# Graph layer on one core: VectorE's first gate of a node block moved up, one eviction per turned tile pair, and the first edge group started among the counting tiles

## What is computed

```python
h = relu(layernorm(x))                                  # every node
w = relu(edge_feat @ W_fc1) @ W_fc2                     # every edge, 224 weights
xs, xv = (h_s @ W_nl0)[dst], (h_v @ W_nl1)[dst]         # gathered node rows
tp = products of w, xs, xv and the edge's direction     # 96 scalars, 128 vectors
agg = segment_sum(tp, src) / 32                         # messages added per node
out_s = agg_s @ W_out_s + h_s @ W_skip0
out_v = agg_v @ W_out_v + h_v @ W_skip1
out = x + concat(silu(out_s[:, :64]), sigmoid(out_s[:, 64:96]) * out_v)
```

## Time and profile before

| | us |
|---|---|
| median of 3 runs | 1428.96 (1420.41 to 1432.81) |
| the profiled execution | 1418.56 |
| its span | 1416.7 |
| counting tiles, about | 0 to 195 |
| edge groups, about | 195 to 660 |
| start of the node stage, about | 660 to 700 |
| node rounds, about | 700 to 1408 |

### The profile page before, as it was taken

The page is one execution under the profiler, slowest core; times in us unless marked ns, Lnnn a source line. Parts: engine busy times, 40 slices in busy tenths (PEclk is TensorE's granted clock), DMA queues, the critical chain, the costliest instruction groups (busy, mean ns, idle before and its releaser), DMA issues.

```text
span 1416.7 us, 33669 instructions
## 1 busy us (share of the span) xinstructions
PE 1222.7 (86%) x8853; PEld 1006.4 (71%) x8853; DVE 1115.9 (79%) x4156; ACT 1028.6 (73%) x2594; POOL 854.8 (60%) x1077
## 2 busy tenths in 40 slices
PE   4999979988888888895798898899898999888896
PEld 2555547777777777785677787777787888777786
DVE  7999998777777767778287887788888888787875
ACT  2777766777667767774477786678788888777785
POOL 5555477666667666640675665576666666665661
PEclk9999989999999999998699999999999999999999
DMA  5000013333333333331487787788888888787873
GB/s 197 1 0 0 0 38 92 96 92 87 91 94 96 95 83 90 96 89 48 99 250 226 227 235 218 200 242 243 234 244 238 251 241 250 214 230 222 235 206 103
DMA packets 90933, 212.41 MB, mean 150 GB/s; under 512 B 15031, under 2 KB 56282, under 8 KB 90879
## 3 DMA queue, kind: packets, MB, share of 16 engines
q1 hardware_dynamic: 62462, 155.23, 34.0%
q0 software_dynamic: 28416, 56.56, 18.5%
HBM read 127.73 MB, written 84.00 MB: 149 GB/s over the span
## 4 chain that ended last, share of the span: by engine, by line
PE 42%; ACT 17%; issue 12%; DVE 9%; another core or an unknown queue 5%; ACTq 1%; DVEq 0%; POOL 0%; DMA 0%; POOLq 0%
PE bank L1387 9%; ACT nn L1177 8%; PE bank L1379 7%; PE bank L1401 6%; PE bank L1307 4%; PE bank L1336 3%; PE bank L1391 2%; PE bank L1324 2%; PE bank L1320 2%; DVE n_stat L855 2%; PE bank L1322 2%; ACT tpt L1136 2%; PE bank L1291 2%; PE bank L1292 1%
## 5 line engine op out<-in xcount | busy, mean ns | idle before, releaser
L574 POOL DMA_INDIRECT mg<-messages,slot_m x392 | 456.6, 1165 | 281.5 <-ACT slot_m L1199 115.4
L1177 ACT ACTIVATE nn<-xb,n_bias,n_rstd 128x160 f32<-128x160 f32 x686 | 340.5, 651 | 10.9 <-DVE n_bias L656 10.7
L1387 PE MATMUL bank<-wsk_a,nt_a 128*128 128x160 f32 x1568 | 300.1, 315 | 9.9 <-DVE ob L946 7.5
L946 DVE SCALAR_TENSOR_TENSOR ob<-sg,bank 128x128 f32<-128x128 f32 x588 | 132.4, 279 | 154.3 <-ACT ob L1193 150.6
L502 POOL DMA_INDIRECT xg<-x,dst_g x200 | 208.4, 1042 | 61.8 <-issue 56.7
L1387 PEld LDWEIGHTS bank<-wsk_a,nt_a 128*128 128x128 f32 x1568 | 233.5, 197 | 14.9 <-issue 12.7
L1379 PE MATMUL bank<-ident,nn 128*128 128x128 f32 x784 | 149.4, 314 | 78.8 <-ACT nn L1177 55.7
L1379 PEld LDWEIGHTS bank<-ident,nn 128*128 128x128 f32 x784 | 110.8, 210 | 134.7 <-issue 76.3
L855 DVE BATCH_NORM_STATS2 n_stat<-xb 128x6 f32<-128x160 f32 x784 | 200.8, 309 | 1.4 <-DMA xb<-x 1.4
L1401 PE MATMUL bank<-mg,hot 64*128 64x192 f32 x1568 | 186.3, 355 | 8.9 <-issue 4.5
L1184 ACT ACTIVATE nt_a<-bank 128x512 f32<-128x512 f32 x196 | 117.1, 598 | 84.3 <-PE bank L1380 77.8
(11 more groups left out here) (179 smaller groups left out, 2633.8 us busy)
## 6 DMA issues: line engine op xcount, KB each, us to landing
xb<-x SPq DMA_DIRECT2D x97, 640.0 KB
out_dram<-ob SPq DMA_DIRECT2D x97, 640.0 KB
messages<-msg SPq DMA_DIRECT2D x50, 390.6 KB
mg<-messages,slot_m POOLq DMA_INDIRECT x392
ef<-edge_feat_t SPq DMA_DIRECT2D x50, 125.0 KB
xg<-x,dst_g POOLq DMA_INDIRECT x200
xb<-x SPq DMA_DIRECT2D x1, 420.0 KB
out_dram<-ob SPq DMA_DIRECT2D x1, 420.0 KB
```

The costliest lines, as they stand in the source:

```text
L574: pool.indirect_dma_start(mg[:, m, k, :], None, messages[:, :], bass.IndirectOffsetOnAxis(ap=slot_m[:, m, k:k + 1], axis=0)).then_inc(n.g[ ...
L946: last = dve.scalar_tensor_tensor(out=o[:, :, S + V * j:S + V * j + V], in0=sg[:, h, :, :], scalar=1.0, in1=z[:, :, part], op0=ALU.add, op ...
L1177: last = act.activation(nn[:, u % 2, h, :, g % 4], xb[:, u, g, :], ACT.Relu, bias=n_bias[:, u // U, c:c + 1], scale=n_rstd[:, u // U, c:c ...
L1387: pe.matmul(z[:, t, 0:F], nt_a[:, h, t * P:(t + 1) * P], wsk_a[:], start=(t % 2 == 0), stop=False, skip_group_check=True)
```

## The change

It has five parts.

- **VectorE, node stage.** In `round_n` the call `gate(i, u, 0)` moves from behind the statistics (and, in root rounds, behind the whole root chain) to the place between the one-hots and the statistics.
- **ScalarE, both stages.** The turned rows get one PSUM range of five 128-column slots and one SBUF tile, so one copy of 640 columns (`nt`) replaces 512 plus 128, and one of 625 (`ht`) replaces 500 plus 125.
- **First edge group.** Its turn, hidden layer, weights and row products move into the last 20 counting tiles, in PSUM bank 3, which is free there. ScalarE's three evictions go with them.
- **GpSimd.** The four gathers of edge group 2 are issued among the first 20 counting tiles, not after the last.
- **VectorE, edge stage.** `table()` moves from round 0 to round 3.

```diff
@@ node stage, VectorE
+                        if every:
+                            places(i)
                         if extract:
                             seed(j, w)
+                        gate(i, u, 0)
+                        if extract:
                             if measure:
                                 stats_n(s, v, 0, 1)
                             root_a(j, w, 0)
...
-                        if every:
-                            places(i)
-                        gate(i, u, 0)
                         if extract:
                             shift_n(j, w)
@@ node stage, ScalarE
-                        act.activation(nt_a[:, h, :], q_t[h], ACT.Relu)
-                        act.activation(nt_z[:, h, :], q_tz[h], ACT.Relu).then_inc(n.ht, 1)
+                        act.activation(nt[:, h, :], q_t[h], ACT.Relu).then_inc(n.ht, 1)
@@ edge stage, ScalarE
-                        act.activation(ht[:, c, :], p_t, ACT.Copy)
-                        act.activation(hz[:, c, :], p_tz, ACT.Copy).then_inc(e_ht, 1)
+                        act.activation(ht[:, c, :, :], p_t, ACT.Copy).then_inc(e_ht, 1)
@@ edge stage, VectorE
-                    if isinstance(q, int) and q == 0:
+                    if isinstance(q, int) and q == 3:
                         table()
@@ counting tiles, GpSimd
+                        if isinstance(t, int) and t < BR:
+                            gathers(2, 2, [k // BATCH])
...
-                gathers(2, 2)
@@ counting tiles, ScalarE
+                    if isinstance(t, int) and t == NT - BR:
+                        act.wait_ge(e_t, 1)
+                        act.activation(ht[:, 0, :, :], f_t, ACT.Copy).then_inc(e_ht, 1)
+                    if isinstance(t, int) and t == NT - BR + 8:
+                        act.wait_ge(e_h1, 1)
+                        act.activation(hid[:], f_h, ACT.Relu).then_inc(e_hid, 1)
+                    if isinstance(t, int) and t == NT - 3:
+                        act.wait_ge(e_w, 1)
+                        act.activation(w_sb[:, 0, :, :], f_w, ACT.Copy).then_inc(e_wsb, 1)
@@ counting tiles, PE
+                    if isinstance(t, int) and t == NT - BR:
+                        turn_first()
+                    if isinstance(t, int) and t == NT - BR + 12:
+                        hidden_first()
                 edge_tiles(pe, tile_b)
                 for t in range(NT - BLOCK, NT):
                     table(t, t % BR, t // BR)
+                    if t == NT - 8:
+                        weights_first()
+                rows_first()
                 pe.wait_ge(b_free, 3)
```

More of the change, by code:

```diff
@@ L199, in gnn_layer @@
         hot = sb("hot", [P, 2, BPM, P])
-        nt_a = sb("nt_a", [P, 2, 4 * P])
-        nt_z = sb("nt_z", [P, 2, P])
+        nt = sb("nt", [P, 2, 5 * P])
         sg = sb("sg", [P, 2, 4, V])
@@ L496, in _, with gathers @@
                                    pattern=[[1, ET]], channel_multiplier=-1).then_inc(s_const, 1)
[L497 removed]
+                def gathers(q, b, tiles=range(GE)):
                     wait(pool, e_norm, q - D + 1)
@@ L500, in gathers @@
                     pool.sem_inc(s_held, 1)
-                    for t in range(GE):
+                    for t in tiles:
                         pool.indirect_dma_start(xg[:, b, t, :], None, x[:, :],
@@ L781, in products @@
                 def products(p, c):
+                    first = isinstance(p, int) and p == 0
+                    rows = f_x if first else p_x
+                    row_s, row_v = rows[:, :, 0:S], rows[:, :, S:F].rearrange("p t (i k) -> p t i k", i=3)
                     w = w_sb[:, c, :, :]
@@ L1129, in round_e @@
                     c = b % 2
+                    first = isinstance(q, int) and q == 0
                     def take(t):
@@ L1163, in round_e @@
                     take(3)
-                    if within(q):
+                    if within(q) and not first:
                         act.wait_ge(e_w, q + 1)
@@ L1257, in table, with turn_first, hidden_first, weights_first @@
                               skip_group_check=True).then_inc(b_tab, 1)
+                idt = ident[0:ET, 0:ET]
+                def turn_first():
+                    pe.wait_ge(e_norm, 1)
+                    for t in range(GE):
+                        pe.transpose(f_t[:, t, :], hn[:, 0, 0:P, t], idt)
+                    pe.transpose(f_t[:, GE, :], hn[:, 0, P:F, :], idt).then_inc(e_t, 1)
+                def hidden_first():
+                    pe.wait_ge(s_w, 16 * len(weight_loads))
+                    pe.wait_ge(e_f[0], 16)
+                    pe.wait_ge(e_ht, 1)
+                    pe.matmul(f_h, wfc1[:], ef[:, 0, :], start=True, stop=True).then_inc(e_h1, 1)
+                def weights_first():
+                    pe.wait_ge(e_hid, 1)
+                    for t in (0, 2, 1, 3):
+                        part = slice(EF * (t // 2), EF * (t // 2) + EF)
+                        last = pe.matmul(f_w[:, t, :], hid[part, t % 2 * ET:(t % 2 + 1) * ET], wfc2[part, :],
+                                         start=True, stop=True)
+                    last.then_inc(e_w, 1)
+                def rows_first():
+                    pe.wait_ge(e_wsb, 1)
+                    rows(f_x, 0).then_inc(e_xs, 1)
+                def rows(to, c):
+                    for t in range(GE):
+                        pe.matmul(to[:, t, 0:P], ht[:, c, t, :], wnl_a[:],
+                                  start=(t % 2 == 0), stop=True, skip_group_check=True)
+                        if t % 2 == 1:
+                            j = t // 2
+                            last = pe.matmul(to[:, 2 * j:2 * j + 2, P:F], ht[:, c, GE, :],
+                                             wnl_z[:, 2 * V * j:2 * V * j + 2 * V],
+                                             start=False, stop=True, skip_group_check=True)
+                    return last
                 count(0, tri_before, 0).then_inc(b_pre, 1)
@@ L1328, in weights @@
                     def weights(tiles):
-                        if not within(q):
+                        if not within(q) or first:
                             return
@@ L1356, in round_e @@
                     turn(0, p + 1, 1 - c)
-                    if within(q):
+                    if within(q) and not first:
                         wait(pe, e_px, q)
-                        for t in range(GE):
-                            pe.matmul(p_x[:, t, 0:P], ht[:, c, t * ET:(t + 1) * ET], wnl_a[:],
-                                      start=(t % 2 == 0), stop=True, skip_group_check=True)
-                            if t % 2 == 1:
-                                j = t // 2
-                                last = pe.matmul(p_x[:, 2 * j:2 * j + 2, P:F], hz[:, c, :],
-                                                 wnl_z[:, 2 * V * j:2 * V * j + 2 * V],
-                                                 start=False, stop=True, skip_group_check=True)
-                        last.then_inc(e_xs, 1)
+                        rows(p_x, c).then_inc(e_xs, 1)
                 groups(pe, round_e)
```

43 lines of the change are left out of this document (20 added, 23 removed).

## The result

The change made the kernel slower: 1473.01 us (1467.57 to 1477.99, 4 runs) against 1428.36 (1420.41 to 1432.81, 4 runs), a ratio of 1.032 with a 95% interval of 1.026 to 1.038. The profiled execution took 1477.99 us with a span of 1476.2, 59.5 us more than the span before.

A forecast was written before the change was run, and what follows sets the result against it. No engine is full, so waits decide, mostly in the node stage. Terms -7.5 - 24 - 4.9 - 3 - 2 = -41.4 us from 1418.56 give 1377.2; with half the median's 10.4 us offset kept, 1382 us, range 1366 to 1415.

The forecast's parts named there:

- The pauses: Node stage: ScalarE's idle times of 3.0 to 4.2 us behind long gate waits lose three quarters of 32 us, -24 us.
- The pauses stay: Rival: the gate waits go, but ScalarE's pauses come from something else and remain; 1411 us, chance 0.28.
- VectorE becomes late: Rival: in root rounds the waiting gate delays shift and `nn`, and such waits bring more pauses; 1466 us, chance 0.05.
- The gate waits: Node stage: PE's 19 waits of `skip` for VectorE's gate, 6.9 us, go with their hand-overs, -7.5 us.
- The merged eviction: Node stage: one ScalarE eviction for two saves 0.05 us on the loop in each of 98 rounds, -4.9 us.
- Edge groups and seam: Edge groups: merged eviction, -3 us; seam between counting tiles and edge groups: `products` of group 0 near 203 us, -2 us.

The follow-up runs named there:

- held gathers: Kernel before, with GpSimd's gathers of block j also waiting for VectorE's one-hots of block j-2: 1313.9 us, ratio 1.000, on a chip without pauses.
- the gate alone: Kernel before with only the gate's move: 1304.36 us (ratio 0.993) on a chip without pauses, 1475.31 us (1.026) on one with pauses.
- all but the gate: Changed kernel with the gate's move undone: 1310.25 us (ratio 0.998) on a chip without pauses, 1462.92 us (1.014) on one with pauses.

## Why the prediction was wrong

**The pauses: the step that failed.** I read them as set off by PE's long wait for the gate, because each stood behind such a wait, and took three quarters of 32 us as a gain. The waits went, and the pauses went from 6 to 17. With the disturbed and the undisturbed chips side by side the term can be sized, from first to last slot row. Undisturbed, this is 645.9 us for the change and 663.8 for the kernel before with held gathers, which is as fast as the kernel before:

```profile
L1201 ACT ACTIVATE slot_m<-slots_i x98: 189/206/228, 612.2 to 1276.0; 128x4 int32 x80, 128x4 int32<-128x4 int32 x18
```

So the pauses cost the change 762.9 - 645.9 = 117.0 us, and the kernel before 708.8 - 663.8 = 45.0. The term is +72 instead of -24. On a chip with pauses, but without gathers, the change takes 1336.8 - 681.4 = 655.4; the 9.5 us over 645.9 lie at the start of the node stage, where the stop behind the first 16 gathers is. If the kernel before loses as much there, 35.5 us are left for its rounds, where I had 32: the size before was about right, its cause was not.

The rows of before could have told me. A pause stood behind each of six gate waits of 0.45 to 0.95 us (three of them stand under another releaser, though `skip` starts 0.15 us behind the gate's end), but others of 0.48 and 0.51 had none of 3 us or more. The `skip` at 860.04 has one behind it, the one at 1154.32 has not:

```profile
860.04 0.78 PE L1387 MATMUL bank<-wsk_a,nt_a 128*128 128x160 f32 x4 [0.45 <-DVE ob L946]
...
1154.32 0.78 PE L1387 MATMUL bank<-wsk_a,nt_a 128*128 128x160 f32 x4 [0.51 <-DVE ob L946]
```

And the earlier trace rows have 30.5 us of idle time of `ht` under "remote" in the edge groups, where there is no gate. Only one core runs, and on the chip without pauses the changed kernel has no such row. The long gate wait and the pause were two things in one place, behind a root round. That the root chain brings both by shifting VectorE and the gathers against PE is my reading; no run shows it. I gave "no semaphore ties the pause to the gate" to the rival as an argument and then still gave it 0.28 against 0.53.

**The rivals.** "The pauses stay" (1411) was nearest in its reasoning, and too mild: it had them unchanged. "VectorE becomes late" gave 1466, close to the measured 1473, but by another way. Its first half, shift and `nn` late behind a waiting gate, did not come: in the root round of the timeline above the shift ends at 1034.23 and `nn` starts at 1034.49, 0.60 us behind its eviction as in any round, and on chips without pauses every round is 6.8 us, root rounds too. Its second half, more pauses, it tied to these late shifts, which did not come. That 1466 lies near the result is luck. The rule of the Trainium skill ("TensorE: Matmul & The Clock Gate", "Architectural detail: the array is 16× 32×32, not 1× 128×128") on strict order in VectorE's queue, which spoke against the change, brought no loss here: VectorE waits for Silu in front of the statistics, and without pauses the rounds are shorter all the same.

**The gate waits: right, where nothing disturbs them.** -7.5 forecast; the gate alone is 1313.71 - 1304.36 = 9.4 us faster on the chip without pauses, 8.3 of it in the slot rows (663.8 to 655.5). On a chip with pauses it is 2.6% slower.

**The merged eviction: right in kind, taken at half its size.** The step from eviction to `nn` fell to 0.61 as worked out, but I counted one eviction per round on the loop. Both are on it: the round fell by 0.10, and from the gate alone to the whole change the node rounds fall by 9.6 us on chips without pauses. Slot rows there, of the gate alone and of all but the gate:

```profile
L1200 ACT ACTIVATE slot_m<-slots_i x98: 190/205/214, 612.4 to 1267.9; 128x4 int32 x80, 128x4 int32<-128x4 int32 x18
...
L1211 ACT ACTIVATE slot_m<-slots_i x98: 187/202/211, 610.8 to 1269.9; 128x4 int32 x80, 128x4 int32<-128x4 int32 x18
```

655.5 and 659.1 against 645.9 us. Without the gate's move the evictions give 663.8 - 659.1 = 4.7 us, since root rounds, which then wait for the gate, stay as they are (7.25 and 7.29 us); with it they give 9.6. By the Trainium skill's budget of about 0.3 us per ACTIVATE ("ScalarE: Activation LUTs", "Rules for kernel authors") it would have been several times as much; that row is for a bias given as a pointer, and the kernel gives the evictions none. The rows' 0.05 per eviction held.

**Edge groups and seam: wrong, nothing or worse.** -5 forecast. The first slot row comes at 613.9 instead of 612.4 without pauses (at 610.8 with all but the gate, which has the same edge groups and seam), and at 677.1 instead of 671.7 with them. VectorE's first `products` did come earlier, 204.1 instead of 206.63, but the gain is used up by the first message, which both kernels evict at 216.7 us. Line of `products` and of the message, changed kernel:

```profile
L795 DVE TENSOR_TENSOR w4xv<-w_sb,bank x48: 545/547/555, 204.1 to 638.4; 125x384 f32<-125x384 f32 x48
...
L1158 ACT ACTIVATE msg<-bank x100: 537/544/562, 216.7 to 662.8; 125x448 f32<-125x448 f32 x100
```

and of the message before:

```profile
L1143 ACT ACTIVATE msg<-bank x100: 537/544/565, 216.7 to 657.4; 125x448 f32<-125x448 f32 x100
```

The eviction of 625 columns takes 0.69 us as worked out, but it is not on the path. A stretch of the edge groups on the chip without pauses (gate alone) shows the bound:

```profile
300.00:350.00 50.00, 49.85 (x410) 44.25 (x411) 43.62 (x158) 40.59 (x91) 40.26 (x46) 1.00 0.40 109
```

PE is busy for 49.85 of 50 us, and for 391 of 400 from 200 to 600 us. In the profile that I predicted from it had 407 of 465 us. I took the rest for waits of the streams; since the chip without pauses has almost none of it, most must be the late signals, though no run took the gathers out of the edge groups.

**The sum by measured terms**: gate -8.3, evictions -9.6, pauses +72.0 and what lies before the node rounds +5.4 give the 59.5 of the spans. The pauses' term is what is left over in the node rounds, so that the sum closes proves nothing. Of the 5.4 the chips without pauses show nothing clear: first slot rows at 610.8 and 613.9 around 612.2.

## What to carry to other kernels

An idle time that no semaphore explains has an unknown cause, and its place behind another wait is no evidence that removing this wait removes it; its forecast is a range in both signs, and such a pause grows as easily as it shrinks when streams shift against each other. Before a loop is tightened that has a chain of GpSimd gathers beside a dense PE, take the gathers out once and look whether the pauses go. And where a kernel has such pauses, measure on more than one chip: here the gate's move and the rest of the change were each a gain on one chip and a loss on another.

## What the runs showed of the hardware

The same kernel takes 1312 to 1315 us on some chips and 1427 to 1438 on others, each with little scatter. Of the 104.6 us between two of its profiled spans (1416.7, and 1312.1 with held gathers) 45.0 lie between the slot rows and 59.5 before them. In the node stage it is one effect: on the slower chips, ScalarE and, where the rows show it, GpSimd go on up to 4 us, once 8 to 9, after the matmul whose semaphore they wait for has ended by its row. PE goes on for 2 to 3 us meanwhile and then stops as well, and VectorE's signals come through (in the pause shown, its residual ends at 1036.58 and SyncE's store of it starts at 1036.76). With the gathers left out, the effect is gone from the node rounds and stays in the edge groups, which keep theirs; so in the node rounds it needs the gathers, as instructions or as transfers. Behind a pause TensorE's granted clock falls to 0.50, the lower level of 1.2 GHz, as this stretch of the changed kernel shows:

```profile
1044.00:1045.00 1.00, 1.00 (x7) 1.00 (x5) 1.00 (x2) 0.96 (x2) 0.69 (x2) 0.50 0.00 0
```

which costs that round another 1.5 us (8.3 instead of 6.8). What holds the signals back, why only some chips do it, why a root round attracts it on the unchanged schedule, and why either half of the change brings more of it, is open. No version was found that is faster than the kernel before on both kinds of chip.
